# Experts' numbers of the small tiles kept in registers, and the last but one tile finished earlier

## The reference

```python
logits = xf @ w_router
probs = softmax(logits, axis=-1)
topk_w, topk_idx = top_k(probs, 2)          # 8 experts
weights = sum(topk_w[..., None] * one_hot(topk_idx, 8), axis=1)
h = gelu(einsum('te,ieh->tih', xf, w1) + b1)    # 256 -> 1024
out = einsum('tih,ihe->tie', h, w2) + b2        # 1024 -> 256
x = x + tanh(g_ffn[0]) * sum(out * weights[..., None], axis=1)
```

## Time and profile before

| | us |
|---|---|
| median of 3 runs | 703.63 |
| lowest and highest run | 702.64 and 705.05 |
| the profiled execution | 703.17 |
| its span in the trace | 700.2 |
| TensorE busy in the span | 658.5 (94%) |
| VectorE, ScalarE, GpSimd busy | 483.5, 343.9, 304.9 |
| share of the full TensorE clock granted over the span | 0.99 |

### The profile page before, as it was taken

The page is one execution under the profiler, slowest core; times in us unless marked ns, Lnnn a source line. Parts: engine busy times, 40 slices in busy tenths (PEclk is TensorE's granted clock), DMA queues, the critical chain, the costliest instruction groups (busy, mean ns, idle before and its releaser), DMA issues.

```text
span 700.2 us, 21600 instructions
## 1 busy us (share of the span) xinstructions
PE 658.5 (94%) x6779; PEld 578.0 (83%) x6780; DVE 483.5 (69%) x1328; ACT 343.9 (49%) x771; POOL 304.9 (44%) x420
## 2 busy tenths in 40 slices
PE   7999999999999998999999999999999989888882
PEld 6799999999999996998989899898999766666661
DVE  5678888888877966787656556565565566666662
ACT  4677777777777845332423334233343334343430
POOL 6323677677775547734323323233232423232222
PEclk9999999999999999999999999999999999999997
DMA  5243454554543554245323232332332322222211
GB/s 194 61 143 107 151 183 138 171 158 145 176 161 122 158 178 125 78 126 108 45 52 46 47 58 40 53 45 49 57 47 51 46 49 36 45 35 45 40 17 22
DMA packets 51321, 63.20 MB, mean 90 GB/s; under 512 B 4577, under 2 KB 46951, under 8 KB 51111
## 3 DMA queue, kind: packets, MB, share of 16 engines
q1 hardware_dynamic: 37695, 43.94, 21.1%
q0 software_dynamic: 13440, 18.14, 15.3%
q10 hardware_dynamic: 104, 0.04, 0.0%
HBM read 37.39 MB, written 24.63 MB: 89 GB/s over the span
## 4 chain that ended last, share of the span: by engine, by line
PE 48%; issue 4%; DVE 4%; POOL 3%; ACTq 1%; ACT 1%; DMA 1%; DVEq 0%; POOLq 0%
PE banks L1699 16%; PE banks L1677 15%; PE banks L1716 8%; PE banks L1738 7%; POOL routed L795 2%; PE banks L1689 1%; POOL l_exp L778 1%; ACT stage L953 1%; ACTq L624 1%; DVE prob L1232 1%; PE banks L1728 1%; DMA out_dram<-prob_t,meta 1%; DVE prob_t L1250 0%; DVE prob_t L1254 0%; DVE xn_t L1239 0%
## 5 line engine op out<-in xcount | busy, mean ns | idle before, releaser
L938 ACT ACTIVATE stage<-banks,bias_t 128x256 f32<-128x256 f32 x200 | 83.9, 470 | 169.3 <-PE banks L1677 169.3
L1677 PE MATMUL banks<-xn_t,w_hi 128*128 128x256 f16 x800 | 133.5, 274 | 1.4 <-DVE xn_t L1239 1.4
L1699 PE MATMUL banks<-w,prob 128*128 x800 | 132.4, 273 | 0.7 <-DVE v_area L1264 0.7
L832 POOL DMA_INDIRECT out_dram<-prob_t,meta x46 | 73.2, 1592 | 118.5 <-DVE prob_t L1254 104.3
L1677 PE MATMUL banks<-xn_t,w_lo 128*128 128x256 f16 x400 | 109.5, 274 | 0.0
L1699 PE MATMUL banks<-w,v_area 128*128 x400 | 109.0, 273 | 0.0
L953 ACT ACTIVATE stage<-banks,bias_t 128x128 f32<-128x128 f32 x168 | 52.6, 363 | 91.5 <-PE banks L1716 91.4
L1716 PE MATMUL banks<-xn_t,w_hi 128*128 128x128 f16 x672 | 75.5, 219 | 17.1 <-ACT stage L953 17.1
L1716 PEld LDWEIGHTS banks<-xn_t,w_hi 128*128 x672 | 56.1, 98 | 41.6 <-issue 24.3
L1677 PEld LDWEIGHTS banks<-xn_t,w_hi 128*128 x800 | 78.4, 98 | 11.3 <-issue 2.0
L1699 PEld LDWEIGHTS banks<-w,prob 128*128 128x128 f16 x800 | 78.1, 98 | 9.7 <-issue 0.8
(11 more groups left out here) (250 smaller groups left out, 1327.3 us busy)
## 6 DMA issues: line engine op xcount, KB each, us to landing
stage<-in_L_ffn_w_dram SPq DMA_DIRECT2D x32, 512.0 KB, 4.0
x_row<-routed SPq DMA_DIRECT2D x25, 265.0 KB, 2.8
x_in<-in_x_dram SPq DMA_DIRECT2D x16, 256.0 KB, 3.6
x_res<-in_x_dram SPq DMA_DIRECT2D x16, 256.0 KB, 4.1
out_dram<-x_res SPq DMA_DIRECT2D x16, 256.0 KB, 2.7
x_row<-routed SPq DMA_DIRECT2D x21, 132.5 KB, 2.1
routed<-pad_rows SPq DMA_DIRECT2D x9, 265.0 KB, 3.8
out_dram<-prob_t,meta POOLq DMA_INDIRECT x67, 3.8
```

The lines of the kernel that those rows point to most:

```text
L832: pool.indirect_dma_start(out[:, :], bass.IndirectOffsetOnAxis(ap=meta_of(j, pj)[:, b, E:E + 1].bitcast(U32), axis=0), y[:, pj, b], None, ...
L938: ins = act.activation(hid[:, c], H[:, q, c % PER * SLOTS:(c % PER + 1) * SLOTS], ACT.Gelu_apprx_tanh, bias=k.bias_t[:, bass.ds(e * HC + c ...
L1677: mm = pe.matmul(H[:, q, c % PER * SLOTS:(c % PER + 1) * SLOTS], w[:, bass.ds(e, 1), i, c * P:(c + 1) * P].rearrange("p a n -> p (a n)"), ...
L1699: mm = pe.matmul(Y[pj][:, b * D:(b + 1) * D], h[:, pj, c, b * P:(b + 1) * P], w[:, bass.ds(e, 1), c, :].rearrange("p a n -> p (a n)"), sta ...
```

## The change

1. `LOOP_TILES` ends at tile 20 and not 22, so that the full tiles 20 to 24 are written out.
2. A new function `small_experts` loads the small tiles' experts during those five tiles and keeps them in registers. ScalarE and VectorE load four or five ahead of each tile's work, 21 in all; TensorE loads one after each bank of the first layer, two after the first bank of tile 20. The loads in the small tiles' steps go: two per step on TensorE, one each on ScalarE and VectorE.
3. In step 45 TensorE does two `c` of tile 44's second layer after each of the first four `c` of tile 45's first layer, and none after the last four. VectorE finishes tile 44 after the second bank's split of tile 45 and not after the fourth.

```diff
                     mm.then_inc(k.v_done, 1)
 
 
-LOOP_TILES = range(8, FULL_TILES - 3 - (FULL_TILES - 3) % 2)
+LOOP_TILES = range(8, FULL_TILES - 5 - (FULL_TILES - 5) % 2)
 assert EARLY_TILES < LOOP_TILES.start and LATE_FULL >= 0 and FULL_TILES % 2 == 1
 
 
@@ -623,6 +623,13 @@
                 eng.wait_ge(plan, PLAN_OPS)
             return eng.value_load(k.expert_of[0:1, bass.ds(tile, 1)], min_val=0, max_val=E - 1)
 
+        def small_experts(eng, kept, tile, q=0, parts=1):
+
+            if isinstance(tile, int) and LOOP_TILES.stop <= tile < FULL_TILES:
+                at = (tile - LOOP_TILES.stop) * parts + q
+                for small in range(FULL_TILES + at, MAX_TILES, (FULL_TILES - LOOP_TILES.stop) * parts):
+                    kept[small] = expert(eng, small)
+
         late_meta = top[:].rearrange("p i n -> p (i n)")[:, 0:2 * SB * (E + 1)].rearrange(
             "p (j b n) -> p j b n", j=2, b=SB)
 
@@ -961,9 +968,12 @@
                     ready(act, x_lo_sb, t - 1)
                     act.activation(small_x_hi[t % 2], X_T[:, 0:KC * P], ACT.Copy).then_inc(x_hi_sb, 1)
 
+                experts = {}
+
                 def step(m, par):
                     j, mj, pj = item(m, par, 0)
                     if tile_exists(j):
+                        small_experts(act, experts, j)
                         e = expert(act, j)
                         for q in range(HID_BANKS):
                             gelu(j, e, q)
@@ -973,9 +983,8 @@
                         if small_exists(j):
                             high_small_rows(j)
                     elif small_exists(j):
-                        e = expert(act, j)
                         for q in range(HID_BANKS):
-                            gelu_small(j, e, q)
+                            gelu_small(j, experts[j], q)
                             if q == 1 and small_exists(j + 1):
                                 high_small_rows(j + 1)
 
@@ -1270,7 +1279,7 @@
 
                 def finish_small_rows(t):
                     p, h, b = small_turn(t)
-                    e = expert(dve, t)
+                    e = experts[t]
                     ready(dve, y_ps, t)
                     if t < FULL_TILES + 2:
                         dve.wait_ge(added[p], 16 * SB * len(range(p, FULL_TILES, 2)))
@@ -1287,9 +1296,12 @@
                     dve.tensor_scalar(y[:, p, 0], y[:, p, 0], small_meta(t)[:, bass.ds(e, 1)], k.gates[:, 1:2],
                                       ALU.mult, ALU.mult).then_inc(y_sb, SB)
 
+                experts = {}
+
                 def step(m, par):
                     j, mj, pj = item(m, par, 0)
                     if tile_exists(j):
+                        small_experts(dve, experts, j)
                         for q in range(HID_BANKS):
                             split_hidden(j, pj, q)
                         j, mj, pj = item(m, par, 1)
@@ -1302,10 +1314,12 @@
                             split_small_hidden(j, q)
                             if q == 1 and small_exists(j + 1):
                                 low_small_rows(j + 1)
+                            if q == 1 and j == MAX_TILES - 1:
+                                finish_small_rows(j - 1)
                     j, mj, pj = item(m, par, -1)
                     if tile_exists(j):
                         finish_rows(j, mj, pj)
-                    if small_exists(j):
+                    if small_exists(j) and j != MAX_TILES - 2:
                         finish_small_rows(j)
 
                 def low_values():
@@ -1741,27 +1755,29 @@
                     if c == HC - 1:
                         mm.then_inc(y_ps, 1)
 
+                experts = {}
+
                 def step(m, par):
                     j, mj, pj = item(m, par, 0)
                     if tile_exists(j):
                         e = expert(pe, j)
                         for q in range(HID_BANKS):
                             first_layer(j, e, q)
+                            small_experts(pe, experts, j, q, HID_BANKS)
                         j, mj, pj = item(m, par, 1)
                         if tile_exists(j):
                             turn_tile(j, mj, pj)
                         if small_exists(j):
                             turn_small(j)
                     elif isinstance(j, int):
-                        if small_exists(j):
-                            e = expert(pe, j)
-                        if small_exists(j - 1):
-                            e_before = expert(pe, j - 1)
                         for c in range(HC):
                             if small_exists(j):
-                                first_small(j, e, c)
-                            if small_exists(j - 1):
-                                second_small(j - 1, e_before, c)
+                                first_small(j, experts[j], c)
+                            if small_exists(j - 1) and j != MAX_TILES - 1:
+                                second_small(j - 1, experts[j - 1], c)
+                            if j == MAX_TILES - 1 and c < HC // 2:
+                                second_small(j - 1, experts[j - 1], 2 * c)
+                                second_small(j - 1, experts[j - 1], 2 * c + 1)
                             if c == 3 and small_exists(j + 1):
                                 turn_small(j + 1)
                     j, mj, pj = item(m, par, -1)
```

## The result

The changed kernel took 686.22 us (median of 4 runs, 684.62 to 689.09) where the kernel before took 704.34 beside it. The ratio is 0.9744, with a 95% interval of 0.9693 to 0.9794: 18.1 us faster, where 22 were forecast. Measured again in a later series on one chip it was 682.55 against 703.42 us, ratio 0.9716 (0.9695 to 0.9737).

A forecast was written before the change was run, and what follows sets the result against it. Small tiles were taken as bound by TensorE's queue, held 1.4 us a step by two register loads. From 703.17 us, -24.7 - 0.65 - 2.3 + 6.1 = -21.55 gave 681.6 us, range 676.5 to 689.

The forecast's parts named there:

- the first rival: Small tiles: VectorE sets the pace, its finish, splits and x_lo coming late; 685.4 to 692 us, chance 0.20.
- 19 small steps: Small tiles: without the loads each step falls from 6.85 to 5.55 us, near the array's own 5.50; -24.7 us.
- full tiles 20 to 24: TensorE's 21 added loads outrun the queue's lead: 1.1 us lost per tile, 1.75 in tile 20; +6.1 us.
- tile 25: One load goes from ahead of its first layer, so the gap of 0.97 us shrinks; -0.65 us.
- to the last scatter: From tile 45's start to the last scatter 11.8 us in place of 14.1, saving the landing wait; -2.3 us.
- a demand of 8.7 us against a supply of 7.63: Full tile up to its second layer: PE queue's time with four more loads against its lead plus array work.
- four banks of 1.07: Full tile's first layer: PE queue's time per bank, 1.07 us, read from semaphore instructions a bank apart.
- The second rival: Full tiles: the loads are hidden because the queue's lead exceeds 1.95 us; 675.5 us, chance 0.08.
- the third: Full tiles: loads not hidden at all (13.7 for 6.1 us), or VectorE's make x_lo late; 689.2 us, chance 0.11.
- tile 44's allows it at 7.25 + 4.53: Last tiles: tile 44's scatter goes 7.25 us after tile 45's start, letting the last one go 4.53 later, at 11.8.
- the fourth rival: Small tiles: PE's gap is ScalarE's and the loads stand in its shadow; steps stay 6.85, 707.0 us, chance 0.03.
- the fifth: Small tiles: the registers are not kept and nothing changes; chance 0.02.

The follow-up runs named there:

- the runs with five and ten loads: Changed kernel with TensorE keeping full tiles' own expert in tiles 20 to 24, 682.12 us; changed kernel with each of TensorE's 21 small-tile loads doubled, 697.64 us.
- the run with one load: Kernel before, with TensorE keeping a small tile's register from its first layer's step for its second layer, one load per step left: 693.42 us.

## Why the prediction was right, and which terms were off

It forecast 681.6 us in a range of 676.5 to 689, and 686.22 lies in it. The mechanism held and a size was off. The median lies above the forecast's own band, 678 to 685, and among the times that the first rival would give (685.4 to 692). So the time doesn't decide between the two; the steps of 5.50 us do. Of the 4.6 us missed, 2.9 are the terms below. The other 1.8 are not among them; the kernel before, beside it, also took 1.2 more than the 703.17 that the forecast started from. That 682.55, in the later series, lies inside the band is luck as well, since the terms are the same. The terms, from the traces:

| term | forecast | measured |
|---|---|---|
| 19 small steps | -24.7 | -25.7 |
| full tiles 20 to 24 | +6.1 | +8.9 |
| tile 25 | -0.65 | -0.26 |
| to the last scatter | -2.3 | -1.8 |
| from it to the end | 0 | +0.2 |
| sum | -21.55 | -18.7 |

**Small steps.** Right. The forecast gave 5.55 for slips that didn't come; the array's 5.50 was the whole of it. x_lo ended 4.4 us into the step, where 4.9 was reckoned; with the forecast's 0.2 us to a matmul the first rival (VectorE paces) had 0.9 us against it and not 0.4.

**Full tiles: the mis-sized term.** The account set a demand of 8.7 us against a supply of 7.63. The supply was right; the demand was 9.1. From the queue's rows the loads are 0.65 each, as forecast, but "four banks of 1.07", taken from one pair of rows, come to (7.2 - 4 x 0.65) / 4 = 1.15 each, 0.3 more in all. The kernel before had it too. Its queue's semaphore instructions in the full tile of the earlier trace rows, one ahead of each bank and one ahead of the transposes, are 4.5 us apart from first to last:

```profile
L107 PEldq EVENT_SEMAPHORE  x5: 51/51/51, 516.8 to 521.3; - x5
```

And the load after the transposes takes 572 ns itself where 300 was read, another 0.27. The transposes took 0.2 less than set (the two loads around them start at 520.9 and 521.7, 0.65 of it the first load). 9.1 - 7.63 = 1.5 a tile, as seen in tiles 21 to 23; tile 24 lost 1.7, since 10.70 stood there. Tile 20 lost 2.6 where 1.75 was forecast; beside its extra load two of its loads took longer, as the rows show (shortest, middle and longest of three, in ns):

```profile
L624 PEldq TENSOR_LOAD <-expert_of x3: 297/480/611, 494.0 to 497.1; - x3
```

Where an account's two sides differ by a seventh (8.7 and 7.63), an error of 5% in one of them is more than a third of the result: the price per load was right and the loss per tile was not. The second rival (a longer lead) and the third's price of nothing hidden (13.7 us) are both out by the runs with five and ten loads, and its other half, a late x_lo, by the run with VectorE's loads moved.

**Tile 25.** From its start to tile 24's second layer 3.88 us were to become 3.23; they became 3.58 (552.93 to 556.51):

```profile
556.51 0.44 PE L1713 MATMUL banks<-w,prob 128*128 x2 [0.51 <-issue]
...
L107 PEldq EVENT_SEMAPHORE  x1: 51/51/51, 551.0 to 551.0; - x1
...
L624 PEldq TENSOR_LOAD <-expert_of x1: 310/310/310, 555.6 to 555.6; - x1
```

The load's 0.65 went, and the lead is 1.9 us again (551.0 to 552.93), as forecast. But the queue's work from there to the load took 4.6 us where 4.3 had been read from the kernel before: the same error as in the full tiles, a queue time taken from one execution of a stretch. With tile 24's load gone as well there is no gap, 8.16 us.

**The last tiles.** The step that failed is "tile 44's allows it at 7.25 + 4.53". Tile 44's rows were ready at 672.73, 6.45 us into the step, as reckoned (6.5), but its scatter went out at 8.04, held by the landing of tile 43's. That one had gone out at 3.49 (669.77), and scatters stand 4.3 to 4.6 us apart: 3.49 + 4.55 + 4.26 = 12.30. Tile 45's rows, ready at 676.60, held nothing:

```profile
672.32 0.41 DVE L1296 TENSOR_SCALAR prob_t<-prob_t,meta,gates 128x256 f32<-128x256 f32 x1
...
676.19 0.41 DVE L1296 TENSOR_SCALAR prob_t<-prob_t,meta,gates 128x256 f32<-128x256 f32 x1
```

The forecast followed the chain of landings back by one link and it had two. Before the change tile 43's scatter lay 6.8 us ahead of tile 44's and held nothing. Steps of 5.50 leave about 1 us of slack a scatter, and a landing can take longer than that. In the run with VectorE's loads moved, tile 43's scatter goes out 6.1 us after tile 42's (664.38), and all three last ones wait for a landing:

```profile
670.51 1.56 POOL L825 DMA_INDIRECT out_dram<-prob_t,meta  x1 [4.35 <-DMA out_dram<-prob_t,meta]
675.15 1.57 POOL L825 DMA_INDIRECT out_dram<-prob_t,meta  x1 [2.88 <-DMA out_dram<-prob_t,meta]
679.71 1.55 POOL L825 DMA_INDIRECT out_dram<-prob_t,meta  x1 [2.99 <-DMA out_dram<-prob_t,meta]
```

That makes 13.32 us, where the nine profiles of kernels with both parts of the change lie between 12.30 and 13.32. In the run with the loads moved alone, tile 43's scatter waits as well, but there it costs nothing, since tile 44's goes out only when its own rows are ready.

**Slower than before** (the fourth rival) and **nothing changes** (the fifth) are decided by the run with one load and by the steps of 5.50.

## What to carry to other kernels

A register load on TensorE is free only as long as the queue's lead lasts: write down the queue's time (loads, addresses, semaphores) beside the array's for each stretch between two points where the lead is full, and move the loads to the stretch with the most spare, here the second layer, not just out of the tight loop. When supply and demand come out within some 15% of each other, take the demand from all the rows of a stretch and not from one pair. Where DMAs wait for the landing of the one before, a faster loop removes their slack, so follow that chain back until a link has some.

## What the runs showed of the hardware

- TensorE's queue entered a full tile and tile 25 1.9 us ahead of the array, before and after the change, some 18 matmuls of 0.109 us. What limits it was not separated.
- The same load took 302 ns as a rule. In the changed kernel the one after the transposes took 597, 572, 573 and 555 ns in tiles 21 to 24, and two in tile 20 took 611 and 480. In the kernel with doubled loads, whose queue had no lead either, none in tiles 21 to 24 took over 311. What the long ones hit is open.
- A register load among TensorE's matmuls cost 0.57 to 0.74 us each once the lead was used up, in the kernel with doubled loads even where its register was never used.
- The attention, untouched, took 259.7 to 266.1 us to the first full tile in the thirteen profiles of this case. It moves the spans by more than several of the differences told here; so times from tile 20 on are compared.
- The table of waits named ScalarE for 16.3 us that were the queue's, and VectorE's split for a gap in which the queue was loading a register.
